# One slot later for the channel attention's projection, and the second LayerNorm's transposes in pairs

## The chip, the cores and the metric

The kernel runs on one core of a Trainium2 chip. The metric is device time in microseconds, median of the runs; lower is better. The engines of the core are TensorE (PE), VectorE (DVE), ScalarE (ACT), GpSimd (POOL) and SyncE (SP, which issues the DMAs). Each works through its own instructions in their written order and waits on semaphores.

## The reference

Input x has 32 images of 192 channels and 32 x 32 positions (1024 tokens). Cut to what matters:

```python
x = x + proj(channel_attention(x))       # 8 heads of 24 channels; softmax over 24 x 24 logits, q and k normalised
t = tokens(x)                            # (32, 1024, 192)
t = t + causal_attention(layernorm(t))   # 6 heads of 32, softmax over 1024 keys, scale 1/sqrt(192)
h = bitlinear(layernorm(t), W1, b1)      # 192 -> 768, weights +-1 by group, activations clipped
h = gelu(h)                              #   and scaled by the absolute maximum of a group of 6 images
t = t + bitlinear(h, W2, b2)             # 768 -> 192
```

A group's absolute maximum must be known before its activations are scaled, so each bitlinear needs a pass over the whole group before anything is scaled. Images come in five groups of six; two more are left, which the last bitlinear leaves at zero.

## The kernel before

**Attention stage.** For each image the causal attention is cut into 48 units (six heads by eight query tiles of 128), one unit per slot; a group has 6 x 48 slots. In slot n, PE multiplies the scores of unit n into one half of `S` (L669, then the mask at L671), DVE takes the row maxima (`nmax`, L1203), ACT the exponentials into `work` (L926). Three slots later PE transposes the exponentials into the two banks of `PT` (L683), DVE copies the first four blocks out (L378) and ACT the rest (L930). PV products go to `OUT` (L703). Every twelve slots ACT copies `OUT` to `oT` (L918), PE transposes it back (L712, slot 19 and every twelfth behind it), and DVE divides by the row sums and adds to `T` (L1189 to L1197). Scores of slot n wait for the exponentials of slot n-2, since `S` has two halves, and a transpose waits until its `PT` bank has been copied out.

**Front.** Beside it runs the front of the next image: transposes of x, Gram matrix, channel attention, layernorm, q, k and v of the causal attention. It is cut into steps with two banks in turn, `FR` and the upper half of `S[:, 0]`. Each step has a slot in the table `SLOTS`; small parts of DVE and ACT are in `SMALL_SLOTS`. A step stands behind its slot's scores, transposes and PV products on its engine. The steps here: `attn` (slot 17.5) is DVE's scaling of the channel attention's exponentials (L1116, L1119), which ACT makes in `xexp` (slot 17, L854). `u` (PE L603, copy by ACT L872) multiplies the attention with the projection, `mt` (PE L608, DVE L1125 adds the identity and the bias) folds the value weights in, and `t0` to `t3` (PE L615, L616, copies by ACT L875) apply the result to x, two token tiles each. `ln_stats0` is DVE's statistics of the first four tiles (L1066, L1070). SP loads the next x when t3's matmuls are done. There are 32 fronts, 31 of them inside the attention stage.

**Pass 1.** Behind the attention of a group, the second layernorm and the first bitlinear's maxima are made image by image. PE multiplies six tiles m of 128 hidden channels by 1024 tokens into the halves of `S` (`y1`, L770 adds the bias, L772), DVE takes each tile's absolute maximum (L1237). Between them PE makes the transposes of the next image's normalised tokens (`turn_z2`, L644) in four quarters: 0 and 2 into `FR`, 1 and 3 into `OUT`; quarters 0 and 2 wait for POOL's low parts (L523), ACT copies each quarter out (L909). The same iteration does the statistics of the image after that on DVE (behind the maxima 1 and 2) and their aggregation (L1179, behind maximum 3), POOL turns these into scale and offset (L514 to L519), ACT normalises and rounds (L899, L903), POOL makes the low part. A loop covers five images of a group, the sixth has no transposes beside it.

Of the kernel before, what the change touches and what calls it, by code (L numbers as in the profile page):

```python
# [141 lines left out]
def freed(step):  # L142
# [8 lines left out]


SLOTS = {"xt0": 0, "xt1": 1, "xt2": 2, "xt3": 4, "g0a": 5, "g0": 6, "g1a": 7, "g1": 8, "wg0": 9, "wg1": 10,
         "na": 11, "rb": 15, "u": 18, "mt": 19, "t0": 20, "t1": 21, "t2": 22, "t3": 23, "z0": 31, "z1": 32,
         "z2": 33, "z3": 34, "qk0": 35, "qk1": 36, "qk2": 37, "qk3": 38, "qk4": 39, "qk5": 40, "v0": 41, "v1": 42,
         "v2": 43, "v3": 44}

SMALL_SLOTS = {"norms": 12, "rdiag": 13, "logits": 16, "xexp": 17, "attn": 17.5, "ln_stats0": 22, "ln_stats1": 25,
               "ln_norm0": 27, "ln_norm1": 28, "ln_round0": 28.5, "ln_round1": 29}


def hybrid_kernel(nc, x, wa, wb, wv, wpt, bp, temp, w3, w1, b1, w2, b2, out):
# [5 lines left out]
    with ctx:  # L168
# [3 lines left out]
        def sem(name):  # L172
            return ctx.enter_context(nc.semaphore(name))
# [145 lines left out]
        z2t_made = sem("z2t_made")  # L319
# [63 lines left out]
        def alone(e):  # L383

            e.sem_inc(passed, 1)
# [156 lines left out]
        def _(pe):  # L542
# [96 lines left out]
            def turn_z(bank, k, zc=zcat):  # L639

                v = bank.bitcast(F16).rearrange("p (j n) -> p j n", j=4)
                for t in range(2):
                    for j in range(3):
                        last = tr(v[:, j, P * t:P * t + P], zc[:, 2 * k + t, P * j:P * j + P], ident16[:, :])  # L644
                return last
# [80 lines left out]
            def ffn1(rhs, bank, i):  # L726
                for j in range(3):
                    last = mm(bank, W1b[:, j, P * (i % 6):P * (i % 6) + P], rhs[:, j, :],  # L728
                              start=(j == 0), stop=(j == 2))
                return last  # L730

            def turn_out(src, hf):
                for c in range(2):
                    for t in range(4):
                        o = 512 * c + P * t
                        last = tr(S[0:CH, hf, o:o + P], src(t, c), ident[:, :])
                return last
# [4 lines left out]
            def group_tail(g):  # L742
                nb = g + 1

                pe.wait_ge(w12_ready, 1)
                pe.wait_ge(exp_made, nb * (GS * UNITS))
                pe.wait_ge(oT_made, nb * (GS * NBI))
                for i in range(2):
                    pe.wait_ge(front_free[i], nb * (GS * FRONT_FREES[i]) + FRONT_FREES[i])
                for st in stacked:  # L750
                    pe.wait_ge(st, nb * (GS * STACKS) + STACKS)
                alone(pe)

                def turn_z2(ab, k):
                    if k % 2 == 0:
                        pe.wait_ge(z2lo_made, ab * 2 + (k // 2 + 3))
                    if k >= 2:
                        pe.wait_ge(z2t_made, ab * 4 + (k - 1))
                    turn_z(ZP[k % 2], k).then_inc(z2t_full, 1)

                def y1(b, ab, ab1):
                    for m in range(MH):
                        if m == 0:
                            pe.wait_ge(z2t_made, ab * 4 + 4)
                            alone(pe)
                        pe.wait_ge(max1_step, ab * MH + g + (m + MH - 1))
                        alone(pe)
                        for hf in range(2):
                            bank = S[:, m % 2, 512 * hf:512 * hf + 512]
                            mm(bank, B1S[:, P * m:P * m + P], onesb[:, :].broadcast_to([P, 512]), start=True, stop=False)  # L770
                            for j in range(3):
                                last = mm(bank, W1b[:, j, P * m:P * m + P], Z2[:, b, hf, j, :], start=False, stop=(j == 2))  # L772
                        last.then_inc(y1_full, 1)
                        if ab1 is not None and 1 <= m <= 4:
                            turn_z2(ab1, m - 1)

                with pe.Fori(0, GS - 1) as b:
                    ab = pe.snap(g * GS + b)
                    y1(b, ab, pe.snap(ab + 1))
                y1(GS - 1, g * GS + (GS - 1), None)  # L780
                pe.wait_ge(max1_step, nb * (GS * MH) + g + MH)
                alone(pe)

                def y(b, ab, hf):

                    for m in range(MH):
                        i = MH * hf + m
                        pe.wait_ge(gelu_made, ab * 12 + (i + 1))
                        ffn1(Z2[:, b, hf], Y[i % 4], m).then_inc(y_full, 1)

                def y2(ab, hf):

                    pe.wait_ge(hlo_made, ab * MH + 3 * (hf + 2))
                    alone(pe)
                    for tp in range(2 * hf, 2 * hf + 2):
                        pe.wait_ge(y2_made, ab * 4 + (tp + 1))
                        for t in range(2):
                            o = P * (2 * (tp % 2) + t)
                            for m in range(MH):
                                for part in range(2):  # L800
                                    last = mm(PT[tp % 2][:, C * t:C * t + C], HS[:, hf, part, m, o:o + P], W2b[:, m, :],  # L801
                                              start=(m == 0 and part == 0), stop=(m == MH - 1 and part == 1))
                        last.then_inc(y2_full, 1)


                y(0, g * GS, 0)
                with pe.Fori(0, GS - 1) as b:
                    ab = pe.snap(g * GS + b)
                    y(b, ab, 1)
                    y2(ab, 0)  # L810
                    y(pe.snap(b + 1), pe.snap(ab + 1), 0)
                    y2(ab, 1)
                ab = g * GS + (GS - 1)
                y(GS - 1, ab, 1)
                y2(ab, 0)
                y2(ab, 1)
                with pe.Fori(0, GS // 2) as b2:
                    ab = pe.snap(g * GS + b2 * 2)
                    for s in range(4):

                        pe.wait_ge(o_step, ab * 4 + (4 * (s // 2) + s % 2 + 3))
                        pe.wait_ge(os_made, ab * 2 + (s + 1))
                        turn_out(lambda t, c: OT[:, s, C * t + CH * c:C * t + CH * c + CH], s % 2).then_inc(ot_full, 1)
                pe.wait_ge(os_made, nb * (2 * GS) + 2)
# [11 lines left out]
        def _(act):  # L836
# [53 lines left out]

            order = list(SLOTS.items()) + [("xexp", SMALL_SLOTS["xexp"])]
            order.sort(key=lambda a: a[1])
# [102 lines left out]
        def _(dve):  # L995
# [147 lines left out]

            order = list(SLOTS.items()) + [a for a in SMALL_SLOTS.items() if a[0] != "xexp"]
            order.sort(key=lambda a: a[1])
# [235 lines left out]
```

## Time and profile before

| | |
|---|---|
| median of 3 runs | 4648.91 us (4644.92 to 6351.21) |
| the profiled execution | 4640.95 us, span 4639.2 us, mean granted clock 0.978 |
| PE, matmuls busy | 4074.3 us (88%) |
| PE, weight loads | 2969.3 us (64%) |
| DVE busy | 3330.0 us (72%) |
| ACT busy | 2692.9 us (58%) |
| POOL busy | 363.6 us (8%) |
| DMA | 160.95 MB, 35 GB/s |

The table's shares are over the whole span; a matmul's end is modelled, so matmuls overlap in the rows and PE's busy time is not time at its peak. In the timelines a row merges instructions of one line and form; its start is that of the first, and the number in brackets is the engine's idle time ahead of it with what ended it. A group of six images takes some 870 us, an image of the attention stage some 106 us.

### The profile page before, as it was taken

What the parts mean: (1) busy time and instruction counts of PE and PEld (TensorE: products, weight loads), DVE (VectorE), ACT (ScalarE), POOL (GpSimd) and SP (SyncE); (2) the same over time, 40 slices, a digit from 0 to 9 for tenths busy, and PEclk for the clock granted to TensorE, in tenths of its full rate; (3) what the DMA queues carried; (4) which work ended last, traced back from release to release, by engine and by line L of the source; (5) the groups of instructions that cost most, each with busy time, mean ns of one, the idle gap of its engine ahead of it and who ended that gap; (6) DMA issues with size and microseconds to landing.
All of it is one profiled execution on the core that took longest, in us unless ns stands there. A gap on an engine that the chain in (4) does not pass through costs nothing.

```text
span 4639.2 us, 114644 instructions
## 1 busy us (share of the span) xinstructions
PE 4074.3 (88%) x39208; PEld 2969.3 (64%) x39208; DVE 3330.0 (72%) x6327; ACT 2692.9 (58%) x5901; POOL 363.6 (8%) x374
## 2 busy tenths in 40 slices
PE   6999888879999888999988879999888999888888
PEld 4667665566766646667665656767646667665665
DVE  5777776767777767777776767777767777776776
ACT  2555556556665655555556555656655555556555
POOL 1000002000000110000002000000110000002000
PEclk8999999999999999999999999999999999999999
DMA  2111111011221101111111011221101111111011
GB/s 70 36 36 36 42 36 28 0 49 36 48 50 36 36 0 42 36 36 36 42 36 28 0 49 36 52 47 36 36 0 42 36 36 36 42 36 28 0 42 42
DMA packets 48635, 160.95 MB, mean 35 GB/s; under 512 B 12420, under 2 KB 12934, under 8 KB 48006
## 3 DMA queue, kind: packets, MB, share of 16 engines
q1 hardware_dynamic: 48134, 154.39, 13.9%
q8 instruction: 300, 4.92, 0.4%
q14 instruction: 201, 1.65, 0.1%
HBM read 28.52 MB, written 25.17 MB: 12 GB/s over the span
## 4 chain that ended last, share of the span: by engine, by line
PE 62%; DVE 15%; issue 14%; ACT 4%; POOL 2%; DVEq 1%; DMA 1%; ACTq 0%; SPq 0%; POOLq 0%
PE PT L683 10%; PE OUT L703 10%; PE S L669 5%; PE PT L801 5%; PE S L728 4%; DVE nmax L1203 4%; DVE work L378 4%; PE S L627 2%; PE FR L627 2%; PE S L772 2%; PE FR L575 2%; PE S L575 2%; DVE XT L1074 2%; PE FR L634 1%; PE S L634 1%
## 5 line engine op out<-in xcount | busy, mean ns | idle before, releaser
L926 ACT ACTIVATE work<-S,nmax 128x256 f32<-128x256 f32 (+7 forms) x1536 | 1138.7, 742 | 1123.6 <-DVE nmax L1203 1059.3
L1203 DVE TENSOR_REDUCE nmax<-S 128x1 f32<-128x256 f32 (+7 forms) x1536 | 1157.6, 754 | 801.1 <-PE S L671 781.3
L683 PE MATMUL PT<-ident,work 128*128 128x128 f32 x6912 | 1103.3, 280 | 222.9 <-DVE work L378 195.1
L683 PEld LDWEIGHTS PT<-ident,work 128*128 128x128 f32 x6912 | 745.1, 142 | 430.7 <-DVE work L378 259.2
L378 DVE COPY work<-PT 128x512 f32<-128x512 f32 (+3 forms) x1536 | 894.4, 582 | 41.6 <-PE PT L683 35.4
L669 PE MATMUL S<-KS,QS 128*128 128x512 f16 (+3 forms) x1152 | 321.9, 334 | 61.6 <-ACT work L926 28.7
L671 PE MATMUL S<-causal,identb 128*128 128x128 bf16 x1536 | 339.1, 221 | 0.0
L669 PE MATMUL S<-odd 128*128 128x512 f16 (+3 forms) x1152 | 315.7, 328 | 23.0 <-ACT work L926 21.6
L930 ACT ACTIVATE work<-PT 128x512 f32<-128x512 f32 (+3 forms) x768 | 331.2, 431 | 3.4 <-PE PT L683 3.4
L703 PE MATMUL OUT<-work,odd 128*32 128x128 f32 x6912 | 304.9, 277 | 0.0
L1237 DVE TENSOR_REDUCE gm<-S 128x1024 f32 (+1 forms) x180 | 220.1, 1223 | 117.4 <-PE S L772 117.1
L703 PE MATMUL OUT<-work,V 128*32 128x128 f32 x6912 | 303.0, 275 | 0.0
L728 PE MATMUL S<-odd,W1b 128*128 (+1 forms) x1080 | 258.0, 391 | 49.5 <-ACT work L969 41.1
L926 ACT ACTIVATION_READ_ACCUMULATOR work<-S,nmax 128x1 f32 x1536 | 301.3, 196 | 0.0
L772 PE MATMUL S<-odd,W1b 128*128 (+1 forms) x1080 | 291.8, 379 | 0.0
L969 ACT ACTIVATE work<-S,sc 128x512 f32<-128x512 f32 x360 | 254.8, 783 | 50.3 <-PE S L728 50.0
L703 PEld LDWEIGHTS OUT<-work,odd 128*32 128x32 f32 x6912 | 236.5, 110 | 39.8 <-issue 30.6
L703 PEld LDWEIGHTS OUT<-work,V 128*32 128x32 f32 x6912 | 234.3, 109 | 39.8 <-issue 32.1
L801 PE MATMUL PT<-W2b,work 128*128 128x192 f16 x2880 | 247.5, 246 | 8.8 <-DVE odd L1290 8.8
L801 PEld LDWEIGHTS PT<-W2b,work 128*128 128x128 f16 x2880 | 238.9, 98 | 23.2 <-DVE odd L1290 9.9
L1282 DVE SCALAR_TENSOR_TENSOR work<-work 128x1024 f16<-128x1024 f32 x180 | 218.3, 1224 | 29.0 <-ACT work L976 24.8
L671 PEld LDWEIGHTS S<-causal,identb 128*128 128x128 bf16 x1536 | 151.5, 99 | 126.3 <-issue 11.4
(205 smaller groups left out, 6005.9 us busy)
## 6 DMA issues: line engine op xcount, KB each, us to landing
X<-in_x SPq DMA_DIRECT2D x32, 768.0 KB, 5.3
odd<-hi_z SPq DMA_DIRECT2D x128, 192.0 KB, 4.2
odd<-odd SPq DMA_DIRECT2D x128, 192.0 KB, 4.2
out_y<-work SPq DMA_DIRECT2D x64, 384.0 KB, 3.6
QS<-hi_z SPq DMA_DIRECT2D x64, 192.0 KB, 4.0
QS<-odd SPq DMA_DIRECT2D x64, 192.0 KB, 4.1
KS<-hi_z SPq DMA_DIRECT2D x64, 192.0 KB, 4.3
KS<-odd SPq DMA_DIRECT2D x64, 192.0 KB, 4.5
```

The source lines that it names most:

```text
L378: copy(PTS[m % 2][:, m // 2 % RING, P * c0:P * (c0 + k)], PT[i % 2][:, 0:P * k]).then_inc(pt_free[i % 2], 1)
L669: mm(S[:, n % 2, c0:min(w, c0 + 512)], q, KS[u % 2][:, h, c0:min(w, c0 + 512)], start=True, stop=c0 + 512 < w)
L671: mm(S[:, n % 2, w - P:w], identb[:, :], causal[:, :], start=False, stop=True).then_inc(scores_full, 1)
L683: last = tr(bank[:, P * (j - c0):P * (j - c0) + P], PS[m % 2][:, m // 2 % 2, P * j:P * j + P], ident[:, :])
L703: last = mm(OUT[32 * hh:32 * hh + 32, o:o + P], V[u % 2][:, j, D * h:D * h + D], PTS[k % 2][:, unit_of(k, hh) // 2 % RING, P * j:P * j + P ...
L728: last = mm(bank, W1b[:, j, P * (i % 6):P * (i % 6) + P], rhs[:, j, :], start=(j == 0), stop=(j == 2))
L772: last = mm(bank, W1b[:, j, P * m:P * m + P], Z2[:, b, hf, j, :], start=False, stop=(j == 2))
L801: last = mm(PT[tp % 2][:, C * t:C * t + C], HS[:, hf, part, m, o:o + P], W2b[:, m, :], start=(m == 0 and part == 0), stop=(m == MH - 1 and ...
L926: A(PS[n % 2][:, n // 2 % 2, 0:w], S[:, n % 2, 0:w], ACT.Exp, bias=nmax[:, n % MAXES:n % MAXES + 1], accum_out=rowsum[:, sum_col(n):sum_co ...
L930: pt_copy(act, lambda o, x: A(o, x, ACT.Copy), g, images, i)
L969: A(H[:, i % MH, :], Y[i % 4], ACT.Gelu, bias=rb1[:, i % MH:i % MH + 1], scale=r1).then_inc(gelu_made, 1)
L1203: v.tensor_reduce(nmax[:, n % MAXES:n % MAXES + 1], S[:, n % 2, 0:P * (qtile(n) + 1)], AX.X, ALU.max, negate=True).then_inc(max_made, 1)
```

## The change

The steps `u`, `mt` and `t0` to `t3` stand one slot later each, on PE, ACT and DVE; so does `ln_stats0`. `attn` stays at 17.5 and `ln_stats1` at 25. In pass 1, the four transposes of the next image stand in two pairs, behind tiles m = 2 and m = 4, instead of one each behind m = 1 to 4. The wait for the copied transposes ahead of an image's first tile is split: the first half of tokens waits for two copies, the second for all four.

```diff
-         "na": 11, "rb": 15, "u": 18, "mt": 19, "t0": 20, "t1": 21, "t2": 22, "t3": 23, "z0": 31, "z1": 32,
+         "na": 11, "rb": 15, "u": 19, "mt": 20, "t0": 21, "t1": 22, "t2": 23, "t3": 24, "z0": 31, "z1": 32,
...
-SMALL_SLOTS = {"norms": 12, "rdiag": 13, "logits": 16, "xexp": 17, "attn": 17.5, "ln_stats0": 22, "ln_stats1": 25,
+SMALL_SLOTS = {"norms": 12, "rdiag": 13, "logits": 16, "xexp": 17, "attn": 17.5, "ln_stats0": 23, "ln_stats1": 25,
...
                         if m == 0:
-                            pe.wait_ge(z2t_made, ab * 4 + 4)
+                            pe.wait_ge(z2t_made, ab * 4 + 2)
                             alone(pe)
...
                         for hf in range(2):
+                            if m == 0 and hf == 1:
+                                pe.wait_ge(z2t_made, ab * 4 + 4)
+                                alone(pe)
...
-                        if ab1 is not None and 1 <= m <= 4:
+                        if ab1 is not None and m in (2, 4):
+                            turn_z2(ab1, m - 2)
                             turn_z2(ab1, m - 1)
```

PE's order in slots 18 and 19 of an image's attention, before (L603 is u, L712 the transposes of `oT`, L608 mt; register instructions are left in):

```order
L683 MATMUL PT<-ident,work 128x128 x7
L358 REGISTER_ALU
L601 REGISTER_ALU
L603 MATMUL FR<-WPT,RD 96x192 x2
L665 REGISTER_ALU
L669 MATMUL S<-KS,QS 128x512
L669 MATMUL S<-KS,QS 128x128
L671 MATMUL S<-causal,identb 128x128
L681 REGISTER_ALU
L683 MATMUL PT<-ident,work 128x128
L710 ISA
L712 MATMUL PT<-ident,oT 128x96 x4
```

and the same place now:

```order
L683 MATMUL PT<-ident,work 128x128 x7
L665 REGISTER_ALU
L669 MATMUL S<-KS,QS 128x512
L669 MATMUL S<-KS,QS 128x128
L671 MATMUL S<-causal,identb 128x128
L681 REGISTER_ALU
L683 MATMUL PT<-ident,work 128x128
L710 ISA
L712 MATMUL PT<-ident,oT 128x96 x4
L358 REGISTER_ALU
L601 REGISTER_ALU
L603 MATMUL FR<-WPT,RD 96x192 x2
```

u has moved behind slot 19's scores, its one transpose and the four of `oT`.

PE's order between mt and t0 before (L683 are transposes, L703 PV products, L615 begins t0):

```order
L608 MATMUL S<-zt,WV 96x192 x2
L665 REGISTER_ALU
L669 MATMUL S<-KS,QS 128x384
L671 MATMUL S<-causal,identb 128x128
L681 REGISTER_ALU
L683 MATMUL PT<-ident,work 128x128 x7
L703 MATMUL OUT<-work,V 32x128 x3
L358 REGISTER_ALU
L615 MATMUL FR<-MT,X 128x192
```

and now:

```order
L608 MATMUL S<-zt,WV 96x192 x2
L665 REGISTER_ALU
L669 MATMUL S<-KS,QS 128x512
L669 MATMUL S<-KS,QS 128x128
L671 MATMUL S<-causal,identb 128x128
L681 REGISTER_ALU
L683 MATMUL PT<-ident,work 128x128 x3
L358 REGISTER_ALU
L615 MATMUL FR<-MT,X 128x192
```

Slot 21's scores and three transposes stand there instead of slot 20's scores, seven transposes and three PV products.

PE's order in the loop of pass 1 from the second tile on, now (L773 and L775 are what L770 and L772 were, L644 the transposes of the next image; before, the first six stood behind the second tile and the next six behind the third):

```order
L773 MATMUL S<-onesb,B1S 128x512
L775 MATMUL S<-odd,W1b 128x512 x3
L766 REGISTER_ALU
L773 MATMUL S<-onesb,B1S 128x512
L775 MATMUL S<-odd,W1b 128x512 x3
L773 MATMUL S<-onesb,B1S 128x512
L775 MATMUL S<-odd,W1b 128x512 x3
L756 ISA
L644 MATMUL FR<-ident,hi_z 128x128 x6
L644 MATMUL OUT<-ident,hi_z 128x128 x6
L766 REGISTER_ALU
```

The third tile has moved ahead of the first pair of transposes.

## Rows read from the trace of the kernel before

**Rows 1.** List of waits, whole run: engine, line, releaser, total, times, longest.

```profile
PE FR L603 <- DVE RD L1119: 48.2, 32, 3.1
...
PE FR L644 <- POOL hi_z L523: 34.4, 20, 1.8
```

**Rows 2.** Timeline of PE, slots 18 to 21, first image: start, duration, line.

```profile
128.26 0.94 PE L683 MATMUL PT<-ident,work 128*128 128x128 f32 x7
130.65 0.89 PE L603 MATMUL FR<-WPT,RD 96*96 96x192 f32 x4 [1.45 <-DVE RD L1119]
131.37 0.44 PE L669 MATMUL S<-KS,QS 128*128 128x512 f16 x2
131.65 0.22 PE L671 MATMUL S<-causal,identb 128*128 128x128 bf16 x1
131.71 0.33 PE L683 MATMUL PT<-ident,work 128*128 128x128 f32 x1
132.28 0.55 PE L712 MATMUL PT<-ident,oT 96*128 96x96 f32 x4 [0.23 <-ACT work L930]
...
134.02 0.33 PE L669 MATMUL S<-KS,QS 128*128 128x384 f16 x1
...
135.45 0.59 PE L615 MATMUL FR<-MT,X 97*128 97x192 f32 x2
...
136.86 0.43 PE L669 MATMUL S<-KS,QS 128*128 128x512 f16 x2
...
137.52 0.49 PE L615 MATMUL S<-MT,X 97*128 97x192 f32 x2
```

**Rows 3.** Timeline of DVE over slots 18 and 19 of the same image.

```profile
129.95 0.16 DVE L1116 RECIPROCAL sc<-sc 96x2 f32<-96x2 f32 x1 [1.68 <-ACT RD L854]
...
130.98 0.68 DVE L378 COPY work<-PT 128x512 f32<-128x512 f32 x1
131.91 0.83 DVE L1203 TENSOR_REDUCE nmax<-S 128x1 f32<-128x640 f32 x1 [0.25 <-PE S L671]
...
134.31 0.61 DVE L1125 TENSOR_TENSOR MT<-S,IADD 97x192 f32<-97x192 f32 x2
```

**Rows 4.** Timeline of PE, the scores of slot 25, same image.

```profile
145.46 0.59 PE L669 MATMUL S<-KS,QS 128*128 128x512 f16 x2
145.89 0.22 PE L671 MATMUL S<-causal,identb 128*128 128x128 bf16 x1
```

**Rows 5.** Timeline of DVE, the maxima of slot 25.

```profile
146.24 1.22 DVE L1203 TENSOR_REDUCE nmax<-S 128x1 f32<-128x1024 f32 x1
```

**Rows 6.** Windows behind u, PE: stretch, us, busy (count), PEclk, DMA share, GB/s.

```profile
237.00:243.00 6.00, 5.77 (x29) 0.72 0.00 1
...
4141.80:4147.80 6.00, 5.76 (x29) 0.72 0.01 1
```

**Rows 7.** Timeline of PE, u of three images in a row, third group.

```profile
1868.62 0.89 PE L603 MATMUL FR<-WPT,RD 96*96 96x192 f32 x4 [1.45 <-DVE RD L1119]
...
1976.54 0.89 PE L603 MATMUL FR<-WPT,RD 96*96 96x192 f32 x4 [1.45 <-DVE RD L1119]
...
2082.78 0.89 PE L603 MATMUL FR<-WPT,RD 96*96 96x192 f32 x4 [1.44 <-DVE RD L1119]
```

**Rows 8.** Timeline of PE, pass 1 of the first group.

```profile
789.17 0.51 PE L644 MATMUL FR<-ident,hi_z 128*128 128x128 f16 x6 [1.67 <-POOL hi_z L523]
789.52 0.38 PE L770 MATMUL S<-onesb,B1S 128*128 128x512 bf16 x1
...
791.24 0.50 PE L644 MATMUL OUT<-ident,hi_z 128*128 128x128 f16 x6
...
802.84 0.51 PE L644 MATMUL FR<-ident,hi_z 128*128 128x128 f16 x6 [1.64 <-POOL hi_z L523]
```

**Rows 9.** Timeline of DVE, the aggregation between them.

```profile
794.96 0.63 DVE L1179 BATCH_NORM_AGGREGATE mv<-stats 128x2 f32<-128x6 f32 x8
```

**Rows 10.** Timeline of POOL, the second low part.

```profile
803.91 1.59 POOL L523 TENSOR_TENSOR hi_z<-XT,hi_z 128x768 f16<-128x768 f32 x1 [1.12 <-ACT hi_z L903]
```

## Prediction

> **What bounds the kernel now.** I read the list of waits first, then the timelines of PE, DVE and ACT around the moved steps, then the granted clock over the stretch behind them, and last the four engines in pass 1. TensorE (PE) is the busiest engine, but it is stopped at fixed places. Two of them are what the change touches: 32 waits of step u's matmuls for DVE, 48.2 us, and 20 waits of pass 1's first transposes for POOL, 34.4 us [rows 1]. The reader should not take the first one as money on the table before seeing what stands behind it.
>
> **Step u, before.** In slot 18 PE ends the seven transposes of tile 15 at about 129.1 (seven at 0.12 us from 128.26) and stands until 130.65, since u needs the channel attention that DVE scales right behind its reciprocal of 129.95 [rows 2, 3]. DVE itself stood 1.68 us for ACT's exponentials until 129.95 [rows 3]. This DVE stop has two followers: u on PE, and DVE's own next work (row maxima of slot 18, then the copy 130.98 to 131.66). The change moves only the first.
>
> **Part A: u, mt, t0 to t3 one slot later, ln_stats0 too.** Nothing is added: the same four u, eight mt and 32 t matmuls, the same ACT copies and DVE adds, per front; 31 fronts run inside the attention stage. No DMA changes its size; the load of the next x waits for t3, so it is issued one slot later, with some twenty slots left before it is used. Step by step for the first image:
> - After tile 15's transposes PE now takes slot 19's scores at once: 0.34 us (131.37 to 131.71), so until about 129.5. Next come slot 19's transpose and the four transposes of oT. The one goes into the bank that DVE's copy empties at 131.66; it started at 131.71 before and it does now. The other waits for an ACT copy that ends after the exponentials of slot 18, and those follow the maxima that follow DVE's stop: 132.28, as before [rows 2, 3].
> - So PE's idle time does not shrink. From 129.1 to 132.28 it did u (0.72), scores (0.34) and one transpose (0.06), and idled 2.05. Now it does the last two and idles 2.77, of which 2.15 in one piece.
> - From 132.28 on PE is never idle until slot 25's scores at 145.46 [rows 2, 4]. In this stretch u's 0.72 us is now additional, in front of slot 20. Slot 24's scores come 0.6 us earlier than before (t3 now stands behind them), but slot 25's come 0.72 later.
> - Who waits there: DVE's maxima of slot 25. They start at 146.24, and the last score matmul was issued at 145.89; maxima follow that by 0.26 (131.65 to 131.91), so 146.15 would have been possible: slack 0.09 [rows 2 to 5]. From there DVE runs on without a PE wait for several slots, so what it starts later it ends later.
> - A new wait: t0 needs the DVE additions of mt. Before, slot 20's scores, seven transposes and three PV blocks stood between (134.02 to 135.45, 1.43 us). Now only slot 21's scores and three transposes do, 0.66 us (136.86 to 137.52), against 0.26 + 0.61 = 0.87 us for the additions [rows 2, 3]. That is 0.2 us of PE standing at t0. Behind it in PE's queue are all scores of slots 22 to 25. The ACT copy of u needs about 0.5 us and has slot 20's scores, transposes and PV (1.4 us) as cover: nothing.
> - Sum: 0.72 + 0.20 - 0.09 = 0.83 us per front, times 31: +25.7 us. Lower bound 0 (the delay lands in some gap that I don't see), upper 1.0 us (31 us).
>
> That a PE delay at this place reaches the end of the image is shown by the granted clock. In 8 of the 31 six-microsecond stretches behind u the mean clock is 0.72 instead of 1.00, a time at half speed (1.2 instead of 2.4 GHz) [rows 6] (the first and the last of the eight). Such an image lasts 107.92 us from u to u (1868.62 to 1976.54), the next without it 106.24 [rows 7]. So a dip costs 1.68 us, and all of it arrives at the end.
>
> **Part A, the clock.** These dips follow the idle stretch around u. It becomes 2.77 us instead of 2.05, with its long piece 2.15 instead of 1.5. More images should then drop to 1.2 GHz. How many no row shows: the bounds are 8 (as now) and 31 (all). With the idle time a third longer I take the middle, 20: 12 more dips at 1.68 us, +20 us; the ends are 0 and +39 us. The Trainium skill (TensorE: Matmul & The Clock Gate, "HAM oscillation") warns only of idle gaps longer than any in this stretch; by that rule no dip would be added and the sum would be 20 us lower. The trace disagrees with it already, since eight dips stand behind gaps of 1.5 us.
>
> **Part B: pass 1's transposes in pairs.** Per group, five iterations transpose the next image; four of them stall, 20 in all [rows 1]. An iteration lasts 13.67 us (789.17 to 802.84), and its PE work is six tiles of 1.72 us and four transposes of 0.35: 11.7 us [rows 8]. The cycle is one of latency: turn0, tile 2, turn1, tile 3, its maximum on DVE, aggregation (794.96 + 0.63 = 795.59), then POOL, ACT, POOL, and turn0 of the next image at 802.84, which is 7.25 us after the aggregation [rows 8 to 10]. Now tile 2 is done before turn0, out of the cycle: T, two transposes to T+0.7, tile 3 to T+2.4, DVE (behind tile 2's maximum and the statistics) reaches tile 3's maximum at about T+2.8, aggregation ends at T+4.6, next turn0 possible at T+11.8. PE's own work, with the small gap at the loop's turn, I put at 11.9. Both limits meet, so the iteration takes 11.9 instead of 13.67: 1.8 us less. turn2 needs POOL's second half, ready at 803.91 + 1.59 = 805.5, 2.7 us after turn0 [rows 10], and stands at T+4.1: no wait. turn3 needs only ACT's second copy, about T+2.6. The new wait ahead of the second half of tile 0 finds the last copy (T+6.3) done, as tile 0 starts at T+6.7.
> The first stalled iteration keeps its chain (turn0 unchanged, tile 2 already done: 1.7 us), the next three give 1.8 each: 7.1 us per group, five groups: -35.5 us. Bounds: 0, if the latency is made up elsewhere, and 39 us, 20 times 1.95 (13.67 less 11.72).
>
> **Sum.** The profiled execution took 4640.95 us (span 4639.2). 4640.95 + 25.7 + 20 - 35.5 = 4651. The median of the three runs is 4648.91, 8 us above the profiled one, so I put the forecast at 4659 us: the two parts nearly cancel, a loss of 0.2%.
>
> **Rivals.**
> - *A's wait really goes.* If DVE's copy of slot 18 did not hold slot 19's transpose, the 1.45 us before u would be filled 31 times: -45 us, with B -80 us: 4569 us. Against it: transpose start 131.71 right behind a copy end of 131.66 [rows 2, 3]. 6%.
> - *A is neutral.* The delay at slot 25 is absorbed and the dips stay eight: 4649 - 35.5 = 4613 us. For it: slot 24's scores and the copies after them are earlier. Against it: [rows 7] show that such delays arrive. 20%.
> - *The clock falls behind every u* (the slower side): 23 more dips instead of 12, 4659 + 18 = 4677 us. Its share decides the sign: with 25.7 us from the shift, the whole is a loss from 6 more dips on (25.7 + 6 x 1.68 = 35.8 against 35.5). For it: the idle piece grows by 0.6 us in every image alike. 18%.
> - *B brings nothing*: another link of the cycle, most likely DVE's statistics ahead of tile 3's maximum, takes the 1.8 us back. 4659 + 35 = 4694 us. 6%.
> - My forecast: 50%.
>
> **How the numbers follow.** The likeliest case is 4659, its own range 4640 to 4672 (A's delay 0.5 to 1.0 us, 8 to 14 dips more). To hold 8 in 10 the range takes in the neutral case and the clock case: 4612 to 4688. About 2% (93 us) is what a measurement of this kernel can tell from no change. Over 2% faster would need more than both waits together (83 us): 1%. Over 2% slower would need 3 us per image: 2%. Within 2%: 97%.
>
> **What would show it.** Right: in slot 19 PE stands about 2.1 us for DVE's copy ahead of one transpose, and u starts after the four oT transposes without a wait; the wait list shows PT L683 for DVE up by some 60 us and FR L603 gone; slot 25's maxima wait for PE; more stretches behind u at a mean clock near 0.7; image period near 107.1 without a dip. In pass 1, 11.9 us per iteration, POOL waits nearly gone. Wrong: an image period under 106.24 us (then A gains), still eight dips, or an iteration over 12.5 us.

## The result, and the profile after

The changed kernel takes 4658.8 us (median of 12 runs, 4654.19 to 4662.47). The kernel before, run beside it, takes 4645.2 us. The ratio is 1.0028, 95% interval [1.0019, 1.0037]: 13.6 us slower, less than the 2% that count as a change here, but clear of the noise. The forecast was 4659 us.

The profiled execution took 4659.4 us. On its page the span has grown by 18 us and PE is 31 us busier, though it executes the same 39208 matmuls; the clock line shows three of its 40 slices below 9, where it showed one before.

```profile
span 4657.6 us, 114699 instructions
...
PE 4105.5 (88%) x39208; PEld 2985.9 (64%) x39208; DVE 3331.3 (72%) x6327; ACT 2693.1 (58%) x5901; POOL 363.2 (8%) x374
...
PEclk7999999989999999999999989999999999999999
```

The list of waits (engine, line, releaser, total, times, longest), before:

```profile
PE PT L683 <- DVE work L378: 195.1, 438, 0.9
```

and after:

```profile
PE PT L683 <- DVE work L378: 255.5, 433, 2.0
...
DVE MT L1129 <- PE S L608: 62.2, 32, 5.3
DVE sc L1120 <- ACT RD L858: 53.0, 32, 1.7
```

Step u's waits for DVE are down from 48.2 us to a single one of 3.1 (the first front's), and PE's waits for POOL ahead of L644 in pass 1 [rows 1] are gone. But PE's wait for DVE's copies has risen by 60.4 us, and its longest from 0.9 to 2.0. DVE's own stop, now 32 times for line L858, is the 53.0 us that it was. So u's wait has moved and grown. DVE's wait for mt's matmuls ahead of its additions has grown too, from 11.7 us (9 times) to 62.2; how much of that is on the path this list does not say.

The place itself, PE's timeline for slots 18 to 25 of the second image. L669 and L671 are the scores, L712 the transposes of `oT`, L603 is u and L615 t0:

```profile
238.05 0.94 PE L683 MATMUL PT<-ident,work 128*128 128x128 f32 x7
239.05 0.45 PE L669 MATMUL S<-odd 128*128 128x512 f16 x2
239.33 0.22 PE L671 MATMUL S<-causal,identb 128*128 128x128 bf16 x1
241.50 0.33 PE L683 MATMUL PT<-ident,work 128*128 128x128 f32 x1 [1.95 <-DVE work L378]
242.06 0.55 PE L712 MATMUL PT<-ident,oT 96*128 96x96 f32 x4 [0.23 <-ACT work L934]
242.44 0.82 PE L603 MATMUL FR<-WPT,RD 96*96 96x192 f32 x4
...
246.24 0.50 PE L683 MATMUL PT<-ident,work 128*128 128x128 f32 x3
246.79 0.59 PE L615 MATMUL FR<-MT,X 97*128 97x192 f32 x2
...
256.13 0.60 PE L669 MATMUL S<-odd 128*128 128x512 f16 x2
256.56 0.22 PE L671 MATMUL S<-causal,identb 128*128 128x128 bf16 x1
```

The scores of slot 19 follow tile 15's transposes at once, and then PE stands 1.95 us for the single transpose, since its bank is emptied by the DVE copy. u follows the four oT transposes without a wait, where mt stood before. The three transposes of slot 21 are issued in 0.33 us, so from 246.57 to 246.79 PE stands ahead of t0. On DVE the maxima of slot 25 now wait:

```profile
256.82 1.23 DVE L1207 TENSOR_REDUCE nmax<-S 128x1 f32<-128x1024 f32 x1 [1.13 <-PE S L671]
```

From the oT transposes to these maxima it is 14.76 us (242.06 to 256.82). Before it was 13.96 (132.28 to 146.24, [rows 2, 5]). That is 0.80 of the 0.85 us that an image grows by.

u of the first three images:

```profile
133.78 0.82 PE L603 MATMUL FR<-WPT,RD 96*96 96x192 f32 x4
...
242.44 0.82 PE L603 MATMUL FR<-WPT,RD 96*96 96x192 f32 x4
...
349.53 1.23 PE L603 MATMUL FR<-WPT,RD 96*96 96x192 f32 x4
```

The first distance is 108.66 us, the second 107.09, against 107.92 and 106.24 before [rows 7]. The windows show which is which (stretch, length, PE busy and count, mean clock as a share of 2.4 GHz, DMA share, GB/s):

```profile
132.40:138.40 6.00, 5.33 (x30) 0.72 0.01 3
241.10:247.10 6.00, 5.33 (x40) 1.00 0.00 1
260.00:266.00 6.00, 5.30 (x49) 0.72 0.15 36
```

The clock fell to 1.2 GHz around the first image's u and not around the second's. Of the 31 such stretches, 23 stand at 0.72 or below and 8 at 1.00; before it was 8 and 23 [rows 6]. Such a stretch is called dipped from here on. The third row shows that the second image's clock does fall, some 19 us behind u, and that this fall costs nothing: the image lasts 107.09 us like those that have no fall at all.

In pass 1, PE's first transposes of two images, and DVE's aggregation between:

```profile
781.20 0.51 PE L644 MATMUL FR<-ident,hi_z 128*128 128x128 f16 x6
781.55 0.50 PE L644 MATMUL OUT<-ident,hi_z 128*128 128x128 f16 x6
...
793.17 0.51 PE L644 MATMUL FR<-ident,hi_z 128*128 128x128 f16 x6
```

```profile
785.29 0.63 DVE L1183 BATCH_NORM_AGGREGATE mv<-stats 128x2 f32<-128x6 f32 x8
```

This iteration is 11.97 us instead of 13.67 [rows 8]. The four distances of the group are 11.98, 11.82, 11.97 and 11.83, 11.90 in the mean; before they were 13.77, 13.66, 13.66 and 13.67, 13.69 in the mean. The aggregation ends at 785.92, 4.72 us after the first transposes; before, that was 6.42 (789.17 to 795.59, [rows 8, 9]). From there to the next first transposes it is 7.25 us, the very number of before.

### The profile page after: what moved, and what is told of

It reads as the page before. It is cut to its first block, busy times and chain, and to the rows that moved or that the text cites. A ratio compares the mean times of both kernels' runs of the same rounds, so it can differ in the third digit from the quotient of the medians.

```text
span 4657.6 us, 114699 instructions
## 1 busy us (share of the span) xinstructions
PE 4105.5 (88%) x39208; PEld 2985.9 (64%) x39208; DVE 3331.3 (72%) x6327; ACT 2693.1 (58%) x5901; POOL 363.2 (8%) x374
## 4 chain that ended last, share of the span: by engine, by line
PE 66%; DVE 15%; issue 12%; ACT 4%; DVEq 1%; DMA 1%; POOL 1%; ACTq 0%; SPq 0%; POOLq 0%
PE PT L683 11%; PE OUT L703 10%; PE S L669 5%; PE PT L805 5%; PE S L728 4%; DVE nmax L1207 4%; PE S L775 4%; DVE work L378 4%; PE S L627 2%; PE FR L627 2%; PE FR L575 2%; PE S L575 2%; DVE XT L1078 1%; PE S L773 1%; PE FR L634 1%
## 5 line engine op out<-in xcount | busy, mean ns | idle before, releaser
L683 PE MATMUL PT<-ident,work 128*128 128x128 f32 x6912 | 1118.4, 283 | 285.4 <-DVE work L378 255.5
L683 PEld LDWEIGHTS PT<-ident,work 128*128 128x128 f32 x6912 | 758.3, 144 | 492.1 <-DVE work L378 314.9
L669 PE MATMUL S<-KS,QS 128*128 128x512 f16 (+3 forms) x1152 | 324.7, 337 | 63.7 <-ACT work L930 29.2
L671 PE MATMUL S<-causal,identb 128*128 128x128 bf16 x1536 | 340.8, 222 | 0.0
L669 PE MATMUL S<-odd 128*128 128x512 f16 (+3 forms) x1152 | 316.8, 329 | 23.6 <-ACT work L930 21.3
L703 PE MATMUL OUT<-work,odd 128*32 128x128 f32 x6912 | 307.0, 278 | 0.0
L703 PE MATMUL OUT<-work,V 128*32 128x128 f32 x6912 | 305.4, 277 | 0.0
L728 PE MATMUL S<-odd,W1b 128*128 (+1 forms) x1080 | 258.2, 391 | 49.6 <-ACT work L973 41.2
L775 PE MATMUL S<-odd,W1b 128*128 (+1 forms) x1080 | 291.9, 379 | 0.0
L703 PEld LDWEIGHTS OUT<-work,odd 128*32 128x32 f32 x6912 | 237.0, 111 | 41.6 <-issue 32.9
L703 PEld LDWEIGHTS OUT<-work,V 128*32 128x32 f32 x6912 | 234.8, 110 | 41.8 <-issue 34.1
L671 PEld LDWEIGHTS S<-causal,identb 128*128 128x128 bf16 x1536 | 152.2, 99 | 127.5 <-issue 13.1
```

The costliest lines, as they stand in the source:

```text
L669: mm(S[:, n % 2, c0:min(w, c0 + 512)], q, KS[u % 2][:, h, c0:min(w, c0 + 512)], start=True, stop=c0 + 512 < w)
L671: mm(S[:, n % 2, w - P:w], identb[:, :], causal[:, :], start=False, stop=True).then_inc(scores_full, 1)
L683: last = tr(bank[:, P * (j - c0):P * (j - c0) + P], PS[m % 2][:, m // 2 % 2, P * j:P * j + P], ident[:, :])
L703: last = mm(OUT[32 * hh:32 * hh + 32, o:o + P], V[u % 2][:, j, D * h:D * h + D], PTS[k % 2][:, unit_of(k, hh) // 2 % RING, P * j:P * j + P ...
```

## Experiments

All ratios are to the kernel before, run on the same chip at the same time, with their 95% intervals. A front is one image's set of steps u to t3; 31 of them run inside the attention stage.

### The two parts apart

The shift alone (pass 1 as before):

```diff
-"u": 18, "mt": 19, "t0": 20, "t1": 21, "t2": 22, "t3": 23 ... "ln_stats0": 22
+"u": 19, "mt": 20, "t0": 21, "t1": 22, "t2": 23, "t3": 24 ... "ln_stats0": 23
```

> Only the six steps u, mt, t0 to t3 and ln_stats0 stand one slot later; pass 1 is as before. Theory (the shift leaves PE behind DVE's stop and costs 0.85 us per front plus more clock dips): 31 x 0.85 = 26 us, 15 more dips at 1.56 to 1.68 us = 23 us, so +49 us on the kernel before, ratio 1.0105; image period 107.1 us without a dip. Rival (the shift is neutral and the pairs bring nothing or cost): +0 to +13 us, ratio 1.000 to 1.003. Rival (only the clock is to blame): +23 us, image period 106.24 without a dip.

Measured: 4694.01 us, ratio 1.0105 [1.0089, 1.0122], 49.6 us more than the 4644.42 beside it. Its distances from u to u are 107.10 without a dip and 108.66 with one, and 23 stretches are dipped. Their sum is 31 x 0.85 + 15 x 1.6 = 50 us. The rival that the shift is neutral is out.

The pairs alone (slots as before):

```diff
-                            pe.wait_ge(z2t_made, ab * 4 + 4)
+                            pe.wait_ge(z2t_made, ab * 4 + 2)
...
+                            if m == 0 and hf == 1:
+                                pe.wait_ge(z2t_made, ab * 4 + 4)
+                                alone(pe)
...
-                        if ab1 is not None and 1 <= m <= 4:
+                        if ab1 is not None and m in (2, 4):
+                            turn_z2(ab1, m - 2)
                             turn_z2(ab1, m - 1)
```

> Only pass 1's transposes stand in pairs, with the split wait; the slots are as before. Theory: five groups at 7.1 us, -35 us, ratio 0.9924; 11.9 us from one first transpose to the next; eight or so dips behind u, image period 106.24. Rival (the pairs bring nothing, the shift is what moved the time): 0 us, ratio 1.000.

Measured: 4610.95 us, ratio 0.9922 [0.9906, 0.9939], 33.5 us less. Together the parts give +49.6 - 33.5 = +16 us, against +13.6 for both at once. Within the intervals, some 8 us either way for each part, the two parts add up.

### Is it DVE's stop that holds PE?

DVE scales the channel attention behind slot 18's maxima and copy instead of ahead of them; all else as in the changed kernel:

```diff
-"attn": 17.5
+"attn": 18
```

> The changed kernel with DVE's scaling of the channel attention at slot 18 instead of 17.5, so behind slot 18's maxima and copy. Theory (what stands ahead of slot 19's transpose is DVE's 1.68 us stop for ACT): the copy of slot 18 ends some 2 us earlier, the four oT transposes start 0.7 us earlier in each image, -22 us on the changed kernel, and fewer dips, another 0 to -24 us: ratio to the kernel before 0.993 to 0.998. Rival (the one-slot shift itself costs through the order of t3 and slot 25's scores, whatever DVE does): same as the changed kernel, 1.003.

Measured: 4604.9 us, ratio 0.9914 [0.9898, 0.9931], 54 us less than the changed kernel, where 22 to 46 were expected. DVE's timeline in slots 18 and 19 of the first image:

```profile
129.82 0.69 DVE L378 COPY work<-PT 128x512 f32<-128x512 f32 x1
130.78 0.16 DVE L1120 RECIPROCAL sc<-sc 96x2 f32<-96x2 f32 x1 [0.27 <-ACT RD L858]
```

The copy now stands ahead of the reciprocal, and the stop is 0.27 us instead of 1.68 [rows 3]. PE's single transpose follows the copy at once, and what it now waits for is ACT:

```profile
130.09 0.45 PE L669 MATMUL S<-KS,QS 128*128 128x512 f16 x2
130.37 0.22 PE L671 MATMUL S<-causal,identb 128*128 128x128 bf16 x1
130.56 0.33 PE L683 MATMUL PT<-ident,work 128*128 128x128 f32 x1
132.29 0.55 PE L712 MATMUL PT<-ident,oT 96*128 96x96 f32 x4 [1.39 <-ACT work L934]
```

The image is 106.28 us without a dip, 0.82 less than with the shift alone, and 7 stretches are dipped instead of 23. The `oT` transposes start 3.20 us behind the first of tile 15's (129.09 to 132.29) instead of 4.01 (238.05 to 242.06), and PE's longest stop is 1.39 us instead of 1.95. 31 x 0.82 + 16 x 1.56 = 50 us, close to the 54 measured. So DVE's stop held slot 19's transpose and, through it, the image.

### The stop taken away at its source

ACT makes the channel attention's exponentials in slot 16, where it idles 1.5 us ahead of slot 17's, instead of behind slot 17's. The idle time, in the trace of the kernel before:

```profile
128.11 1.01 ACT L926 ACTIVATE work<-S,nmax 128x896 f32<-128x896 f32 x1 [1.50 <-DVE nmax L1203]
```

With the pairs, and the steps in their old slots:

```diff
-"xexp": 17
+"xexp": 16
```

> The pairs of pass 1, the slots of before, and ACT's exponentials of the channel attention in slot 16 instead of 17, where ACT idles 1.5 us for slot 17's maxima. Theory (u's wait begins with ACT doing these exponentials behind slot 17's): DVE's stop of 1.68 us is gone, the oT transposes start about 1.3 us earlier, -40 us, the dips behind u mostly go, -13 us, the pairs -35 us: -88 us, ratio 0.981. Rival (another engine takes the 1.3 us back within the image, since DVE is full from slot 25 to 30): only the pairs' -35 us, ratio 0.9924.

Measured: 4552.93 us, ratio 0.9803 [0.9786, 0.9819]. It is the fastest kernel of the study, 92 us below the kernel before and 58 below the pairs alone. DVE and PE, first image:

```profile
129.40 0.28 DVE L378 COPY work<-PT 128x128 f32<-128x128 f32 x1
129.60 0.15 DVE L1120 RECIPROCAL sc<-sc 96x2 f32<-96x2 f32 x1
```

```profile
129.67 0.93 PE L683 MATMUL PT<-ident,work 128*128 128x128 f32 x7
130.44 0.81 PE L603 MATMUL FR<-WPT,RD 96*96 96x192 f32 x4
131.09 0.44 PE L669 MATMUL S<-KS,QS 128*128 128x512 f16 x2
...
132.16 0.55 PE L712 MATMUL PT<-ident,oT 96*128 96x96 f32 x4 [0.46 <-ACT work L934]
...
235.17 0.82 PE L603 MATMUL FR<-WPT,RD 96*96 96x192 f32 x4
```

Neither engine stands ahead of u now, and u starts right behind the transposes in its old slot. What is left is 0.46 us ahead of the `oT` transposes. The image is 104.73 us (130.44 to 235.17), 1.51 less than before, and no stretch around u is dipped. 31 x 1.51 + 8 x 1.68 = 60 us against 58 measured. That fit is partly luck: in five of the 31 images the clock falls at another place, some 29 us behind u, and four of these five lie inside a group and last 106.2 us. Five times 1.46 us are 7, so the sum should be 53, and 5 us stay open. The fall of the second image:

```profile
263.00:269.00 6.00, 5.23 (x43) 0.72 0.01 3
```

### The one-slot shift, without DVE's stop

The same with the steps one slot later (the changed kernel with `xexp` at 16):

> The changed kernel (steps one slot later, pairs) with ACT's exponentials of the channel attention in slot 16: against e5 only the one-slot shift differs, now without DVE's 1.68 us stop. Theory (u's 0.7 us now stands behind the oT transposes, where PE is full up to slot 25, and t0 waits 0.2 us for the additions of mt): 0.8 us per front more than e5, +25 us, and some clock dips that e5 does not have, 0 to +25 us: 4578 to 4603 us, ratio to the kernel before 0.986 to 0.991. Rival (the shift cost only because of DVE's stop): same as e5, 0.980.

Measured: 4575.27 us, ratio 0.9848 [0.9831, 0.9866], 22 us above the kernel with the old slots and just below the expected 4578. From u to u it is 105.57 us (below), against 104.73: 0.84 us, the same price as with DVE's stop. No stretch around u is dipped; four images have the later fall, as five had there.

```profile
132.54 0.55 PE L712 MATMUL PT<-ident,oT 96*128 96x96 f32 x4 [0.48 <-ACT work L934]
132.92 0.82 PE L603 MATMUL FR<-WPT,RD 96*96 96x192 f32 x4
...
238.49 0.82 PE L603 MATMUL FR<-WPT,RD 96*96 96x192 f32 x4
```

So the shift's two costs are separate. The 0.84 us goes with u standing behind the oT transposes, and it is paid with or without a stop ahead. The clock's part at u needs the stop.

### Where the 0.85 us is paid

t3 in slot 25, so that slot 25's scores no longer stand behind it:

```diff
-"t3": 24 ... "ln_stats1": 25
+"t3": 25 ... "ln_stats1": 26
```

> The changed kernel with t3 in slot 25 instead of 24, and its statistics in slot 26: slot 25's scores no longer stand behind t3. Theory (the shift's 0.85 us per front is slot 25's maxima waiting for PE): they start at their old distance, -20 to -26 us on the changed kernel, ratio to the kernel before 0.997 to 0.999, image period 106.2 to 106.4 us without a dip, as many dips as the changed kernel. Rival (all PE work from slot 19 on is on the path, so its order does not matter): same as the changed kernel, 1.003, period 107.1.

Measured: 4666.33 us, ratio 1.0045 [1.0027, 1.0063], 7.5 us above the changed kernel. My expectation failed. DVE's timeline of the second image:

```profile
256.69 1.22 DVE L1207 TENSOR_REDUCE nmax<-S 128x1 f32<-128x1024 f32 x1
...
258.89 0.43 DVE L1207 TENSOR_REDUCE nmax<-S 128x1 f32<-128x256 f32 x1 [0.52 <-PE S L671]
...
263.44 1.25 DVE L1078 TENSOR_SCALAR XT<-T,mv,rstd 128x192 f32<-128x192 f32 x4 [0.56 <-POOL rstd L496]
```

Slot 25's maxima indeed start without a wait for PE. But slot 26's now wait 0.52 us for scores that stand behind t3, and the normalisation waits 0.56 us for POOL, which gets its statistics a slot later. From slot 25's maxima to the normalisation it is 6.75 us (256.69 to 263.44) instead of 5.38 (256.82 to 262.20), and the two waits are 1.08 of the 1.37 us between them. The image takes 107.24 to 107.41 us without a fall at u instead of 107.1, and 26 stretches are dipped: 31 x 0.17 + 3 x 1.56 = 10 us against 7.5 measured. So the earlier maxima are real and the image gains nothing by them. (In 16 images of this trace the clock also falls 22 to 24 us behind u. Dipped images with this second fall last as long as those without it, 108.8 to 108.9 us.) Which of the two new waits alone would be the smaller evil I did not try.

### The clock's share by itself

The changed kernel with matmuls that nobody reads, put where PE stands for DVE's copy:

```diff
+                    if n % UNITS == 19 and n // UNITS < fronts:
+                        wait_freed(pe, g, n // UNITS + 1, "na")
+                        for _ in range(5):
+                            mm(FR[:, :], identb[:, :], onesb[:, :].broadcast_to([P, 512]), start=True, stop=True)
```

> The changed kernel with five added matmuls of 512 columns (1.1 us of work whose result is never read) on PE behind slot 19's scores, where it stands 1.95 us for DVE's copy. They lengthen no path; they only fill the stop. Theory (23 of 31 fronts fall to half the TensorE clock because PE stands there, at 1.56 us each): few or no stretches at 0.72 are left, image period 107.1 us throughout, -20 to -36 us on the changed kernel: ratio to the kernel before 0.995 to 0.999. Rival (the clock falls for another reason, or the fall is hidden): same as the changed kernel or slower, 1.003 to 1.006.

Measured: 4627.67 us, ratio 0.9960 [0.9946, 0.9974], 31 us below the changed kernel. PE, first image (one of the five added matmuls is missing from the trace), and the next two u:

```profile
130.33 1.03 PE L676 MATMUL FR<-onesb,identb 128*128 128x512 bf16 x4
132.22 0.33 PE L687 MATMUL PT<-ident,work 128*128 128x128 f32 x1 [0.86 <-DVE work L378]
...
133.17 0.82 PE L603 MATMUL FR<-WPT,RD 96*96 96x192 f32 x4
...
241.73 0.82 PE L603 MATMUL FR<-WPT,RD 96*96 96x192 f32 x4
...
348.83 0.82 PE L603 MATMUL FR<-WPT,RD 96*96 96x192 f32 x4
```

Useless work made the kernel faster. The wait of 1.95 us is 0.86 now, no stretch around u is dipped, and images last 107.10 us like the undipped ones of the changed kernel. 23 x 1.56 = 36 us would be the whole. Six images still take 108.6 us (the first distance here is one of them), with falls some 28 us behind u that the changed kernel's trace does not have. They take 9 us back, which leaves 27 against the 31 measured. The 107.10 shows that the shift's own 0.85 us is untouched by the clock.

### What in the pairs brings the gain

Pairs behind tiles 1 and 3 instead of 2 and 4, slots as before:

```diff
-                        if ab1 is not None and m in (2, 4):
-                            turn_z2(ab1, m - 2)
-                            turn_z2(ab1, m - 1)
+                        if ab1 is not None and m in (1, 3):
+                            turn_z2(ab1, m - 1)
+                            turn_z2(ab1, m)
```

> The slots of before; pass 1's transposes in pairs, but behind tiles 1 and 3 instead of 2 and 4, with the split wait. Theory (the gain is that tile 2 left the cycle from one first transpose to the next): the cycle again holds two transposes and two tiles, 13.67 us per iteration, ratio 1.000. Rival (pairing itself helps, by fewer changes between kinds of work): as e2, 0.992.

Measured: 4646.96 us, ratio 1.0003 [0.9993, 1.0013].

```profile
788.38 0.51 PE L644 MATMUL FR<-ident,hi_z 128*128 128x128 f16 x6 [1.81 <-POOL hi_z L523]
```

The iteration is 14.00 us (774.38 to 788.38), even longer than the 13.67 expected, and the wait for POOL is back at 1.81. Pairing as such brings nothing; what counts is that tile 2 stands ahead of the first transposes.

One wait instead of two ahead of tile 0, pairs behind 2 and 4:

```diff
                         if m == 0:
-                            pe.wait_ge(z2t_made, ab * 4 + 2)
+                            pe.wait_ge(z2t_made, ab * 4 + 4)
...
-                            if m == 0 and hf == 1:
-                                pe.wait_ge(z2t_made, ab * 4 + 4)
-                                alone(pe)
```

> The pairs behind tiles 2 and 4 with the slots of before, but one wait for all four copies ahead of tile 0, as in the kernel before. Theory (the last copy is done 0.4 us before tile 0): same as e2, ratio 0.992. Rival (without the split the last copy holds tile 0): up to 0.9 us in each of 25 iterations back, ratio up to 0.997.

Measured: 4614.93 us, ratio 0.9933 [0.9915, 0.9950], 4 us above the pairs with the split wait. The intervals overlap, but the traces differ in every iteration: 12.12 to 12.25 us, against 11.82 to 11.98 with the split. In the mean that is 12.2 against 11.9.

```profile
785.40 0.50 PE L644 MATMUL FR<-ident,hi_z 128*128 128x128 f16 x6
...
792.60 0.81 PE L772 MATMUL S<-odd,W1b 128*128 x3 [0.52 <-issue]
...
797.57 0.50 PE L644 MATMUL FR<-ident,hi_z 128*128 128x128 f16 x6
```

```profile
790.93 0.81 ACT L910 ACTIVATE odd<-OUT 128x768 f16 x1
```

ACT's last copy ends at 791.74, a little before PE is through with tile 5, yet PE stands 0.52 us there, which the profile puts down to issue. From that copy's end to this matmul of tile 0 it is 0.86 us. In the two iterations ahead of it, it is 0.88 and 0.87, and in the kernel before, which has the same single wait, 0.77 to 0.93 (796.87 to 797.80 is one). So the distance changes little, which speaks for the copy holding tile 0 although it ends before PE is through; no run tests that by itself. With the split, tile 0's first half goes ahead without it.

## Why the prediction was right, and where not

- **Part A, the path.** u's wait does not become work. Forecast: PE stands about 2.1 us for DVE's copy; measured 1.95, in place of the 1.45 ahead of u before. Forecast +0.83 us per front; the image grew by 0.85 (106.24 to 107.09). The terms are there: u behind the oT transposes (0.72 us, and the shift without the stop costs 0.84 with t0's share), and t0's stop, forecast 0.20, measured 0.22 (246.57 to 246.79). The slot 25 maxima, forecast as the place of payment, start 0.80 later. The list of waits rose by 60.4 us where "some 60" was forecast. The rival that the wait really goes, with its reason turned into an experiment (DVE's copy ahead of the scaling), shows what it would have needed.
- **Part A, the clock.** Forecast: 12 more dips at 1.68 us, +20 us. Measured: 15 more, at 1.56 us in the changed kernel (108.66 against 107.10), 15 x 1.56 = +23. The middle of the bounds was a choice, not a reading. Count and price were off in opposite directions, which is luck. Why the clock falls at 23 places and not at the other 8, which look the same in the timeline, stays open. The rule of the Trainium skill (TensorE: Matmul & The Clock Gate, "HAM oscillation") by which these gaps are too short to matter would have given 20 us less. The trace, and the filled wait above all, decide against it here.
- **Part B.** Forecast 11.9 us per iteration and -35.5 us; measured 11.90 in the mean and, with the pairs alone, -33.5. The reading that the cycle is one of latency was right to the chain: 7.25 us from aggregation to transposes, before and after. The new wait ahead of tile 0's second half was forecast as met, and it is: the last copy ends at 787.55, 6.35 us after the first transposes (forecast 6.3), and the second half starts at 788.60. That the old single wait would have cost 0.3 us per iteration is nowhere in the prediction, and my expectation of that run had it at nothing.
- **The sum.** The forecast of 4659 against 4658.8 is closer than its working, and that is luck. The change was forecast at +10 us and came at +13.6; the kernel before was taken at 4648.91, and with more runs its median is 4645.2. The 3.7 us too high in the one make up for the 3.4 too low in the other. The range given for the likeliest case, 4640 to 4672, is a little wider than its terms give (4642 to 4668).
- **Among the rivals**, A being neutral (20%) is refuted by the shift alone, 1.0105, and B bringing nothing (6%) by the pairs alone, 0.9922. "The clock falls behind every u" came halfway true: 23 of 31, where 20 were forecast.

## What to carry to other kernels

Before moving an instruction away from its wait, look at what else waits for the same thing: here DVE stood for ACT, PE stood for DVE twice, and only one of the two was moved, into a stretch where PE had no room. The remedy was a slot earlier on the engine where the chain begins (one number, 58 us), not a slot later on the one where it ends. In a loop bound by latency, only what is taken out between the cycle's own steps counts; pairing the same work at the wrong place gave nothing.

## What the runs showed of the hardware

A stop of PE of 1.4 to 2 us among dense work lets TensorE's clock fall to 1.2 GHz in some images and not in others: 7 of 31 with 1.39 us in one piece (DVE's scaling at slot 18), 8 of 31 with 1.45, 23 of 31 with 1.95. The whole idle time grew with the longest piece, and no run separates the two. Each of these falls costs 1.5 to 1.7 us of its image (one, whose stretch stands at 0.51, 2.6 us). Filling 1.1 us of the stop with matmuls that nobody reads removed all of them at that place, and the kernel became 31 us faster.

What a fall costs depends on where it lies. Some 28 to 29 us behind u it costs 1.44 to 1.52 us (thirteen images in four runs). In two images of the changed kernel it lies 18.6 us behind u and costs nothing: they last 107.09 us. So the mean clock alone does not give the price of a fall; the length of its image does.
